# Local attention layers: attention weights turned in row halves, and the MLP's 42-row chunk done for two token tiles at once

## The reference

```python
h = shift_token(x)                       # second half of the features from the token before
q, k, v = split(h @ wqkv)                # 8 heads of 64
q, k = rotary_xpos(l2norm(q) * qs, l2norm(k) * ksc)
# window 128: token i sees tokens i-128 .. i
attn = softmax(where(mask, -max, 8 * q @ k.T))
x = x + (attn @ v) @ wo
h = layernorm(shift_token(x)) * lg + lb
a, g = split(h @ w1 + b1)                # 682 hidden units each
x = x + (a * gelu(g)) @ w2 + b2
```

## Time and profile before

| | |
|---|---|
| median of 3 runs | 2332.82 us (2331.42 to 2334.52) |
| the profiled execution | 2333.25 us |
| its span | 2331.4 us |
| busy: TensorE, VectorE, ScalarE, GpSimd | 96%, 70%, 54%, 31% |
| mean granted TensorE clock | 0.989 |
| local layers, about | 1046 to 2331 us |
| chain that ended last, by engine | TensorE 73%, VectorE 14%, DMA 4%, ScalarE 4% |

### The profile page before, as it was taken

The page is one execution under the profiler, slowest core; times in us unless marked ns, Lnnn a source line. Parts: engine busy times, 40 slices in busy tenths (PEclk is TensorE's granted clock), DMA queues, the critical chain, the costliest instruction groups (busy, mean ns, idle before and its releaser), DMA issues.

```text
span 2331.4 us, 42446 instructions
## 1 busy us (share of the span) xinstructions
PE 2239.6 (96%) x16257; PEld 1316.2 (56%) x16306; DVE 1635.1 (70%) x4252; ACT 1254.6 (54%) x2823; POOL 732.4 (31%) x730
## 2 busy tenths in 40 slices
PE   7999999999998999989899999999999999999998
PEld 3333333334634867756566666666666666666665
DVE  6788888886502746668777677677767777787763
ACT  4666666665222622247666656665665665566640
POOL 3344323321111411144433233333333333333321
PEclk7999999999998999999999999999999999999999
DMA  7454343333397020010000000000001000000001
GB/s 240 151 158 121 117 119 122 112 91 109 157 422 297 2 91 19 28 39 3 5 6 6 5 2 6 6 2 32 15 6 53 6 15 24 19 6 24 22 23 40
DMA packets 68617, 158.44 MB, mean 68 GB/s; under 512 B 6256, under 2 KB 49120, under 8 KB 63936
## 3 DMA queue, kind: packets, MB, share of 16 engines
q1 hardware_dynamic: 65856, 146.55, 17.8%
q0 software_dynamic: 2560, 9.18, 1.7%
HBM read 116.39 MB, written 35.13 MB: 65 GB/s over the span
## 4 chain that ended last, share of the span: by engine, by line
PE 73%; DVE 14%; DMA 4%; ACT 4%; issue 3%; POOL 1%; SPq 0%; another core or an unknown queue 0%; POOLq 0%; DVEq 0%; ACTq 0%
PE banks L2073 10%; PE banks L2051 7%; PE banks L1932 6%; PE banks L1946 5%; PE banks L232 4%; PE banks L274 4%; PE banks L2033 3%; PE banks L245 3%; PE banks L1976 3%; PE banks L1991 3%; DMA arena<-in_e_W 3%; DVE arena L483 2%; PE banks L1455 2%; PE banks L1958 2%; PE banks L300 2%
## 5 line engine op out<-in xcount | busy, mean ns | idle before, releaser
L483 DVE TENSOR_REDUCE arena<-banks 128x1 f32<-128x512 f32 x512 | 322.6, 681 | 61.2 <-PE banks L232 60.4
L395 ACT ACTIVATE arena<-banks 128x512 f32<-128x512 f32 x512 | 280.3, 596 | 136.1 <-PE banks L245 112.4
L2073 PE MATMUL banks<-arena 128*128 128x512 f32 x640 | 293.2, 594 | 1.0 <-DVE arena L2258 1.0
L2155 ACT ACTIVATE arena<-arena 128x256 f32<-128x256 f32 (+1 forms) x512 | 286.5, 562 | 5.0 <-DVE arena L2264 4.5
L2411 POOL TENSOR_TENSOR arena<-arena 128x512 f32<-128x512 f32 x128 | 162.8, 1272 | 379.8 <-DVE arena L2295 379.8
L1932 PE MATMUL banks<-arena 128*128 128x512 f32 x512 | 241.5, 594 | 2.8 <-DVE arena L2295 2.8
L232 PE MATMUL banks<-arena 96*128 96x512 bf16 x512 | 202.9, 400 | 14.6 <-DVE arena L483 8.9
L2407 POOL TENSOR_TENSOR arena<-arena 128x16 f32<-128x16 f32 x64 | 189.4, 2959 | 5.4
L2127 ACT ACTIVATE arena<-arena 128x256 f32<-128x256 f32 (+1 forms) x256 | 102.1, 471 | 162.9 <-DVE arena L2240 162.9
L2073 PEld LDWEIGHTS banks<-arena 128*128 128x128 f32 x640 | 115.5, 190 | 126.7 <-issue 116.5
L245 PE MATMUL banks<-arena 128*128 128x512 bf16 x463 | 174.6, 382 | 3.1 <-ACT arena L395 2.2
(11 more groups left out here) (304 smaller groups left out, 4225.7 us busy)
## 6 DMA issues: line engine op xcount, KB each, us to landing
arena<-in_e_W SPq DMA_DIRECT2D x16, 2048.0 KB, 15.6
arena<-stacks SPq DMA_DIRECT2D x64, 384.0 KB, 4.7
arena<-in_e_Wg SPq DMA_DIRECT2D x8, 2048.0 KB, 17.6
stacks<-arena SPq DMA_DIRECT2D x32, 384.0 KB, 2.5
stacks<-arena SPq DMA_DIRECT2D x32, 256.0 KB, 2.8
arena<-dens POOLq DMA_DIRECT2D x32, 256.0 KB, 4.8
arena<-in_xT SPq DMA_DIRECT2D x8, 512.0 KB, 7.8
stacks<-arena SPq DMA_DIRECT2D x32, 128.0 KB, 2.6
```

The costliest lines, as they stand in the source:

```text
L395: e.activation(ex[:, j], self.psum[:, self.exp_bank1(k)], ACT.Exp).then_inc(s["a_e"], 1)
L483: e.tensor_reduce(split(self.maxima[n % 2][:, 0:16], TILES, UNIT)[:, t, j:j + 1], self.psum[:, k % 3], AX.X, ALU.max, negate=True).then_in ...
L2073: i = e.matmul(bank, weights[:, c], self.hT[:, c], start=c == 0, stop=c == 1)
L2155: k = e.activation(pr[:, h, at:], pr[:, h, at:], ACT.Exp, bias=mx[:, h:h + 1], scale=rn[:, h:h + 1], accum_out=den[:, h:h + 1])
```

## The change

- **Layout of the weights.** The division writes not in place but from one raw buffer (`probs[0]`) into a second one (`probs[1]`), where 64-column pieces are ordered (`probs4`) so that a piece of head 0 and one of head 1 lie side by side. Each query half holds three pieces that matter. Maxima wait for the divisions of the tile before.
- **Turning.** `tensor4_weights` now takes a couple of head pairs: 12 transposes of 64 rows by 128 columns (8 in a first tile), alternately of the upper and the lower row half, each half into its own bank. Both couples come before `tensor4_out`. Each bank is copied in one piece of 384 columns, all of couple's even banks by VectorE and odd banks by ScalarE; `pT` has two buffers, so the copies wait for the attend of two tiles back.
- **Values.** As heads lie side by side after the turn, the second head of each pair needs its keys with the 64-row halves exchanged. GpSimd writes each tile's tokens with halves exchanged (`gpsimd4_swap`, four copies of 128x64), and `tensor4_values` runs as 2 x 2 matmuls of 256 columns instead of 2 of 512.
- **Attend.** 64x64 tiles in all tiles of the sequence, both banks summed always, so ScalarE's copy and VectorE's sum (2105, 2269) run in first tiles too.
- **The 42-row chunk.** `gate` and `lin` of chunk 5 put even token tiles into one row half and odd ones into the other. `down` opens tile 2j with five chunks, then tile 2j+1 with five, then does the sixth chunk of both with two matmuls on the two row halves. Each token tile has its own bank, and VectorE adds 256 columns twice.
- One turn of the retention layer on ScalarE is moved behind MLP part 1 in slot 2.

The core of the diff:

```diff
@@ tensor4
-            if c is not None:
-                self.tensor4_weights(e, w, c, 2)
-                self.tensor4_weights(e, w, c, 3)
@@ tensor4_values
-        for c in range(CHUNKS):
-            at = 1 - c + t * P
-            k = e.matmul(self.psum[:, 2], self.xT[:, b, c, at:at + P], self.wqkv4[:, c, 2], start=c == 0, stop=c == 1)
+        w.wait_ge("t_swap", i + 1)
+        out = split(self.psum[:, 2], PAIRS, 2, HD4)
+        for hh in range(2):
+            for c in range(CHUNKS):
+                at = 1 - c + t * P
+                tokens = self.swapped[i % 2][:, c] if hh else self.xT[:, b, c, at:at + P]
+                k = e.matmul(out[:, :, hh], tokens, split(self.wqkv4[:, c, 2], PAIRS, 2, HD4)[:, :, hh], start=c == 0, stop=c == 1, skip_group_check=True)
@@ tensor4_weights
-        for hh in range(2):
-            for n in windows:
-                k = e.transpose(bank[:, hh, n], pr[:, 2 * pair + hh, n * P:(n + 1) * P], self.ident)
-        k.then_inc(self.s["t_pT"], 1)
+        banks = [self.bank4("w", i, 2 * couple + half) for half in range(2)]
+        w.wait_ge("t_pn", 2 * i + couple + 1)
+        w.wait_ge("t_pna", 2 * i + couple + 1)
+        self.emptied4(w, "w", i, 2 * couple)
+        self.emptied4(w, "w", i, 2 * couple + 1)
+        places = [(0, 0, 1), (1, 1, 2), (2, 2, 3)] if i % TILES else [(3, 1, 0), (2, 2, 1)]
+        for n in range(2):
+            for place in places:
+                last = n == 1 and place == places[-1]
+                for half in range(2):
...
+                    rows, at = slice(64 * half, 64 * half + 64), 512 * (2 * couple + n) + P * source
+                    k = e.transpose(banks[half][:, 192 * n + 64 * to:192 * n + 64 * to + 64], self.probs[1][rows, at:at + P], self.ident[rows, rows])
+                    if last:
+                        k.then_inc(self.s["t_pT"], 1)
@@ tensor4_mlp, down
-                for k in range(HID_TILES):
-                    last = k == HID_TILES - 1
-                    at = t % 2 * P if last else t * P
-                    i = e.matmul(bank[:, t % 2 * CH:(t % 2 + 1) * CH], self.hidden[k][:, at:at + P], self.w2[:, k + t // 2 if last else k], start=k == 0, stop=last)
-                i.then_inc(s["m_w2"], 1)
+                for k in range(HID_TILES - 1):
+                    e.matmul(self.bank4(kind, m, index)[:, 0:CH], self.hidden[k][:, index * P:(index + 1) * P], self.w2[:, k], start=k == 0, stop=False)
+                if index % 2 == 0:
+                    continue
+                at = index // 2 * P
+                for half in range(2):
+                    rows = slice(64 * half, 64 * half + 64)
+                    e.matmul(self.bank4(kind, m, index - 1 + half)[:, 0:CH], self.hidden[HID_TILES - 1][rows, at:at + P], self.w2[rows, HID_TILES - 1 + half],
+                             start=False, stop=True).then_inc(s["m_w2"], 1)
@@ scalar4
             if c is not None:
+                self.scalar4_weights(e, w, c, 0)
                 self.scalar4_weights(e, w, c, 1)
             if b is not None:
                 self.scalar4_exp(e, w, b, 1)
-            if c is not None:
-                self.scalar4_weights(e, w, c, 3)
@@ vector4
             if c is not None:
                 self.vector4_weights(e, w, c, 0)
+                self.vector4_weights(e, w, c, 1)
             if a is not None:
                 self.vector4_rotate(e, w, a, 0)
...
-            if c is not None:
-                self.vector4_weights(e, w, c, 2)
@@ vector4_mlp, down
-                    x = self.x_nat[:, b, 2 * pair:2 * pair + 2]
...
+                    for t in (index - 1, index):
+                        x = self.x_nat[:, b, t]
+                        w.wait_ge("m_w2", 4 * m + t + 1)
+                        w.wait_ge("m_bias", m + 1)
+                        e.tensor_tensor(x, x, self.bank4("down", m, t)[:, 0:CH], ALU.add).then_inc(s["m_xw"], 1)
+    def gpsimd4_swap(self, e, w, n):
...
+        if n >= 2:
+            w.wait_ge("t_v", n - 1)
+        for c in range(CHUNKS):
+            at = 1 - c + t * P
+            e.tensor_copy(self.swapped[n % 2][:, c, 0:64], self.xT[:, b, c, at + 64:at + P])
+            k = e.tensor_copy(self.swapped[n % 2][:, c, 64:P], self.xT[:, b, c, at:at + 64])
+        k.then_inc(self.s["t_swap"], 1)
```

More of the change, by code:

```diff
@@ L1728, in gpsimd3 @@
                 self.gpsimd4_rotary(e, w, 0)
+                self.gpsimd4_swap(e, w, 0)
                 self.gpsimd4_tile(e, w, 0)
@@ L1836, in layout4 @@
         self.vn = [r.take(512) for _ in range(4)]
-        self.pT = [split(r.take(512), 2, 2, P) for _ in range(4)]
+        self.pT = [[split(r.take(768), 2, 2, 192) for _ in range(2)] for _ in range(2)]
+        self.swapped = [split(r.take(256), CHUNKS, P) for _ in range(2)]
         self.hn = r.take(1024)
@@ L1848, in layout4 @@
                     uses += [("q", b, 0), ("k", b, 0)]
-                uses += [(kind, m, index) for m, kind, index in mlp_pieces(n, part) if kind != "shift" and (kind != "down" or (kind, m, index) == down_use(m, index))]
+                uses += [(kind, m, index) for m, kind, index in mlp_pieces(n, part) if kind != "shift"]
                 if part == 1 and 0 <= b < TILES4:
@@ L1994, in tensor4_attend @@
     def tensor4_attend(self, e, w, i):
-        first = i % TILES == 0
-        w.wait_ge("t_vn", i + 1)
+        w.wait_ge("t_vn", min(i + 3, TILES4))
         if i:
             w.wait_ge("t_o", i)
-        if not first:
             w.wait_ge("t_x", i)
+        own, ahead = self.vn[i % 4], self.vn[(i - 1) % 4]
         for pair in range(PAIRS):
-            if pair % 2:
-                w.wait_ge("t_pTa", 2 * i + pair // 2 + 1)
-            else:
-                w.wait_ge("t_pTd", 2 * i + pair // 2 + 1)
-            heads = [slice((2 * pair + hh) * HD4, (2 * pair + hh + 1) * HD4) for hh in range(2)]
-            if first:
-                for hh in range(2):
-                    k = e.matmul(self.psum[64 * hh:64 * hh + 64, 5, pair * P:(pair + 1) * P], self.vn[i % 4][:, heads[hh]], self.pT[pair][:, hh, 1],
-                                 start=True, stop=True, skip_group_check=True)
+            w.wait_ge("t_pTd", 2 * i + pair // 2 + 1)
+            w.wait_ge("t_pTa", 2 * i + pair // 2 + 1)
+            pT = self.pT[i % 2][pair // 2][:, pair % 2].rearrange("p a b -> p (a b)")
+            outer, inner = split(pT, 3, 2, 64)[:, 1:3, 0], split(pT, 3, 2, 64)[:, 0:2, 1]
+            for hh in range(2):
+                cols = slice((2 * pair + hh) * HD4, (2 * pair + hh + 1) * HD4)
+                for half in range(2):
+                    rows = slice(64 * half, 64 * half + 64)
+                    near = half == hh
+                    v = own if near or i % TILES == 0 else ahead
+                    k = e.matmul(self.psum[64 * hh:64 * hh + 64, 2 if half else 5, pair * P:(pair + 1) * P], v[rows, cols], outer[rows] if near else inner[rows],
+                                 start=True, stop=i % TILES == 0, skip_group_check=True)
+            if i % TILES == 0:
@@ L2013, in tensor4_attend @@
                 continue
             for hh in range(2):
-                for half, (bank, n) in enumerate(((5, 1), (2, 0))):
+                cols = slice((2 * pair + hh) * HD4, (2 * pair + hh + 1) * HD4)
+                for half in range(2):
                     rows = slice(64 * half, 64 * half + 64)
-                    k = e.matmul(self.psum[64 * hh:64 * hh + 64, bank, pair * P:(pair + 1) * P], self.vn[(i - 1 + n) % 4][rows, heads[hh]], self.pT[pair][rows, hh, n],
-                                 start=True, stop=False, skip_group_check=True)
@@ L2019, in tensor4_attend @@
-            for hh in range(2):
-                for half, (bank, n) in enumerate(((5, 0), (2, 1))):
-                    rows, some = slice(64 * half, 64 * half + 64), slice(64 * half, 64 * half + 64)
-                    k = e.matmul(self.psum[64 * hh:64 * hh + 64, bank, pair * P + 64 * half:pair * P + 64 * half + 64], self.vn[(i - 1 + n) % 4][rows, heads[hh]],
-                                 self.pT[pair][rows, hh, n, some], start=False, stop=True, skip_group_check=True)
+                    near = half == hh
@@ L2024, in tensor4_attend @@
+                    at = 0 if near else 64
+                    k = e.matmul(self.psum[64 * hh:64 * hh + 64, 2 if half else 5, pair * P + at:pair * P + at + 64], (ahead if near else own)[rows, cols],
+                                 pT[rows, 0:64] if near else pT[rows, 320:384], start=False, stop=True, skip_group_check=True)
         k.then_inc(self.s["t_av"], 1)
@@ L2075, in tensor4_mlp @@
                     for half in range(2):
-                        rows, cols = slice(64 * half, 64 * half + 64), slice(256 * half, 256 * half + 256)
-                        i = e.matmul(bank[rows, 0:256], weights[:, c, 0:64], self.hT[:, c, cols], start=c == 0, stop=c == 1, skip_group_check=True)
+                        rows = slice(64 * half, 64 * half + 64)
```

(1 more changed line is left out.)

126 lines of the change are left out of this document (64 added, 62 removed).

## The result

| | before | after |
|---|---|---|
| median, us | 2332.66 (2331.42 to 2334.52) | 2355.44 (2353.76 to 2358.32) |
| profiled execution, us | 2333.25 | 2358.32 |
| its span, us | 2331.4 | 2356.5 |
| ratio to before | | 1.0097, interval 1.0084 to 1.011 |

What follows compares the result with a forecast made beforehand. TensorE's queue was taken as the bound in the local layers, any wait paid in full. Terms 28 - 7 + 0.6 - 1 + 4 + 1.2 = +25.8, called +25, gave 2358 us, range 2327 to 2376.

Steps and rivals of the forecast that it cites:

- Direction and mechanism: Slower, chance 0.76: TensorE waits for VectorE's lin, hT, back and down operations, some 50 slots, 20 to 30 us.
- Part 1: Weights turned in row halves, 0.111 us a round: -0.09 us for 48 tiles, +0.35 for 16, nearly nothing.
- half loads: Rival on the half transposes: rounds of 0.055 us, the skill's 2 times, giving 2339 us; chance 0.09.
- the release: Delay from the end of VectorE's emptying operation until TensorE goes on, taken as 0.05 us.
- Part 2: Couples ahead of the projection: couple 1 waits until VectorE empties its banks, +28 us over 14 groups of four slots.
- A to D: Four kinds of slot, one 128-token tile each, repeating every fourth slot; 2.07 us added per four, 1.91 in layer two.
- Part 3: The 42-row down chunk done for two tiles on row halves: -0.43 us per four slots, -7 us in all.
- Part 4: Values by head parity, +0.6 us in all; GpSimd's swap copies, 0.1 to 0.25 us each, covered by half a slot.
- Part 5: Attend in first tiles, four tiles in the scores' mode: -0.08 us 16 times, -1 us.
- Early slots: First eight slots: couple 1 waits for VectorE's last maximum, 0.5 us each, +4 us.
- Tail: Last two down tiles end together, adding one tile's add, statistics and normalise; the chunk gives back 0.2: +1.2 us.
- The first rival: VectorE releases couple 1's banks before TensorE gets there, so only passes count: put at 2320 us; chance 0.14.

Runs made afterwards that it cites:

- down_alone: The kernel before with only the 42-row chunk done for two token tiles at once, with its banks and adds; 2333.5 us, ratio 0.9999.
- no_swap: The kernel after without GpSimd's swap copies and the values' wait for them, so second heads read wrong keys; 2355.51 us, ratio 1.0102.
- projection_split: The kernel after with half of the output projection ahead of both couples and half behind them; 2330.04 us, ratio 0.9984.
- order_alone: The kernel before with all four head pairs turned by full transposes before the output projection, copies reordered too; 2350.31 us, ratio 1.007.
- couple1_back: The kernel after with couple 1 and its copies moved back behind the output projection; 2319.05 us, ratio 0.9943.
- the two split ones: The kernel after with the projection halved around the couples, 2330.04 us; the same with VectorE's query rotation ahead of its weight copies, 2317.63 us.

## Why the prediction was right, and where its numbers were off

**What bounds the kernel: right.** TensorE's queue is the time; the new idle time, 3.4 us in 100, ate what the passes gave and 1.3 us a period of 80 besides.

**Direction and mechanism: right.** The waits stand in all four kinds of slot, 57 of them, 0.4 to 1.0 us, for the four operations named. They sum to 37.4 us, not 20 to 30, since couple 0 gets over sooner than I took it to (below); the net cost has that saving inside. Busy share in the middle is 96.4, forecast 98. With couple 1 back behind the projection the kernel takes 36 us less.

**Part 1, the price of a round: wrong.** Forecast 0.111, measured 0.062. I took it from a form of plain fp32 matmuls for a transpose, and wrote that a round lasts what the 128 columns of weights need, which would be the same for both. It isn't. The rival named half loads (0.055, chance 0.09) was right on this price, and the Trainium skill's rule that I had set aside (TensorEngine Tiling, Theoretical Speedup: up to 2 times) agrees with 0.062 against 0.110. For plain matmuls a round is 0.112, and no run here has their full-size counterpart. The time wasn't that rival's 2339, since the release, the entering, the chunk and the scores' wait, below, all came out dearer than the sum had them. That the forecast came within 3 us of the result is thus in part luck: a wrong price was made good by what was left out.

**Part 2, per slot.** Forecast A +0.17, B +0.74, C +0.18, D +0.98; measured A -0.03, B +0.54, D +0.88, C and its down chunk together -0.26 against a forecast of +0.18 - 0.34 = -0.16. Several terms were mis-sized and partly cancel. Couple 1 and leaving came to 0.52 (1355.75 - 1355.23) and 0.10, not 0.92: -0.30 a slot. And the release was taken as 0.05 and is 0.15: lin ends at 1354.33 + 0.75 = 1355.08, couple 1 starts at 1355.23; in slot B the hT copy ends at 1375.34, couple 1 starts at 1375.49. That is the 0.1 "for a weight load that nothing hides after the wait", which I had put only into the upper bound: +0.10. And I had left the 0.09 for entering the tiles out of A, B and D: +0.09. The end of the emptying itself was good: 0.86, 1.43, 0.95 and 1.01 after t in A to D, forecast 0.95, 1.52, 0.96 and 1.11. For A that gives 0.17 - 0.30 + 0.10 + 0.09 - 0.09 = -0.03, as measured, and B (0.54) and D (0.88, where couple 1 is 0.19 cheaper, not 0.30) come out likewise. In C the chunk's four records take 0.54 and not 0.43 (1315.14 to 1315.68).

**Part 3, the chunk: the way right, the size not.** Forecast -0.34 in C and -0.09 in B. In C entering and the chunk take 0.09 + 0.54 where 0.86 was, -0.23. In B the chunk takes 0.63 (1382.69 to 1383.32), with 0.09 ahead of it and 0.10 behind, -0.04. That is -4 in all, not -7; alone, with the mode paid everywhere, it comes to nothing (down_alone, -0.6).

**Part 4, values and swap: right.** The swap costs nothing that shows (no_swap). Its copies took 0.23 to 0.7 us each in this trace, not 0.1 to 0.25; the cover held. By the port rule of the Trainium skill (SBUF — State Buffer, two separate sides), an exclusive lock on the pair that VectorE and GpSimd share, the copies could hold VectorE up. From 1300 to 2300 us VectorE is busy 710.1 us with them and 707.6 in no_swap, and the time shows no difference.

**Part 5, attend: nothing.** From the half-chunk of MLP part 1 to the values, slot A takes 3.35 us before (1337.46 to 1340.81) and after (1347.23 to 1350.58); the 0.08 put down for it isn't there.

**Not in the sum.** The scores in slot B wait 0.33 us for the lin of chunk 5, before 0.16: +0.17 a group. The variants that start from after show it (3.5 to 4.5 us in sum, projection_split 14.1), and so does order_alone (4.5); down_alone doesn't (2.1, before 2.3). It enters in slot A already: VectorE's lin behind the projections starts 6.11 us after the MLP piece at 1357.58 (1363.69), before 5.95 us after the one at 1267.83 (1273.78), and that 0.16 stays up to the scores of B. What holds VectorE's chain up there I haven't settled; it isn't the swap.

**The period.** -0.03 + 0.54 - 0.26 + 0.88 - 0.04 (the chunk in B) + 0.17 = 1.26; measured 1.30, forecast 1.6. In the second layer, where D has no back, it is 80.26 against 79.13, +1.13.

**Early slots: too dear.** From the mark to the first transpose of the second slot A it is 140.6 us (1191.61), before 138.1 (1184.35): +2.4, and the first group's own 1.3 is in it. I had taken +4 for the early slots; about 1 is left for them. Couple 1 does wait for the maxima (7.7 us in sum), but there VectorE bounds the slot, and hardly any of TensorE's wait is added to the time.

**Tail: right.** From the start of the last down tiles to the end: 2356.5 - 2337.16 = 19.3, before 2331.4 - 2313.14 = 18.3. +1.1, forecast +1.2.

**Sum.** 2.4 to the second slot A, 15.8 in the 13 periods from there to the last slot A (1191.61 to 2243.30, before 1184.35 to 2220.20), 0.9 from it to the last down tiles, and 1.1 in the tail: 20.3. Forecast: 25.8. Of the 5.5 too much, 3 are the early slots; the rest are the periods, 28 - 7 - 1 + 0.6 = 20.6 forecast against 15.8 + 0.9 and the first group's 1.3.

**The first rival (the bank wait doesn't decide, 2320, chance 0.14)** is refuted as an account of this change: it needed couple 0 to last over 0.95 us, and it lasts about 0.4. But its number is that of the version in which something else covers the emptying: 2319 and 2318.

## What to carry to other kernels

When work is moved across a place where banks come round, find for each bank who emptied it last, when that ends, and count the passes that still lie between; work that was merely next to the wait can have been its only cover. Putting couple 1 back behind the projection turned 22.8 us lost into a ratio of 0.9943, some 14 us gained. Cover can also be split: half of the projection ahead of the transposes hid the emptying and kept one block in tile mode, but gained no more than that (0.9939), and only once VectorE's queue was reordered to match. Take the price of a pass from a form of the same kind of instruction: the records of weight loads (139 against 188 ns) tell kinds apart that the shape doesn't.

## What the runs showed of the hardware

- A pair of fp32 half transposes (64 rows, 128 columns of weights, 64 moving) takes 0.062 us, a full 128x128 transpose 0.110. As plain fp32 matmuls the same pair takes two rounds of 0.112.
- After a wait for a bank, TensorE's first transpose starts 0.15 us after VectorE's operation ended, in all four kinds of slot (A 1355.08 to 1355.23, B 1375.34 to 1375.49, C 1316.63 to 1316.78, D 1336.58 to 1336.73); inside a row of scores it was 0.05 (1368.93 to 1368.98, after).
- A block in tile mode costs about 0.34 us in and out around half transposes (0.09 ahead, 0.15 in it, 0.10 behind) and 0.39 around the chunk in B; a chunk that saves 0.43 us of passes 32 times gave nothing measurable alone.
- Ahead of the mark, the profiled execution of after ran some microseconds at a granted clock of 0.52, where the one of before had 1.00; the window's row (columns as in the earlier trace rows):

```profile
1015.00:1022.00 7.00, 5.91 (x46) 4.96 (x47) 5.50 (x14) 0.60 (x1) 2.00 (x2) 0.52 0.00 0
```

  That is close to the lower of the two levels, 1.2 GHz, in code of the retention layer that the change doesn't touch. It is part of why the mark lies 4.8 us later there: at the pass of line 1517 after is 2.0 us behind (1014.09 and 1016.09), two turns on it is 4.8 (1018.52 and 1023.35). Of the nine traces four, after, couple1_back and the two split ones, have a clock below 0.8 in this window, and the others 1.00, so such a stretch can come or go, and a difference of a few microseconds is read from a mark behind it, with the stretches behind the mark counted too.
